# A fused attention and FFN kernel: TensorE's loop boundary moved behind a projection, two tiles of the next x treated during the value projections, the last set's blocks kept apart

## The reference

```python
q = xn @ Wq;  gate = softmax(xn @ Wg)                       # Wq 512 x 128, three heads
for i in range(3):
    k, v = xn @ Wk[i], xn @ Wv[i]
    w = sigmoid(decay_logits[i]) ** max(s - t - 1, 0) * (s > t)
    blended += gate[..., i:i+1] * (((q @ k.T) * w) @ v)
s = blended @ Wo * out_scale                                 # 128 -> 512
h = silu(xn @ W_gate.T) * (xn @ W_up.T)                      # 512 -> 1376, weights from a table of 16 values
g = silu(h @ W_down.T)                                       # 1376 -> 512
out = x + s * g
```

## Time and profile before

| what | value |
|---|---|
| median of three runs | 1935.36 us |
| profiled execution, its own time | 1939.05 us |
| its span | 1937.2 us |
| TensorE matmul busy | 1826.7 us, 94% |
| VectorE, ScalarE, GpSimd busy | 66%, 41%, 53% |
| mean granted TensorE clock | 0.987 |
| start of groups 4 and 6 (both g = 0) | 586.56 us, 811.62 us |

### The profile page before, as it was taken

How to read it: one execution, slowest core, us unless ns; L and a number is a source line. 1 busy time by engine, 2 the same in 40 slices (tenths; PEclk the granted TensorE clock), 3 DMA queues, 4 the chain that set the end, 5 groups by cost and what they waited for, 6 DMA issues and landing times. The chain is left out here.

```text
span 1937.2 us, 45221 instructions
## 1 busy us (share of the span) xinstructions
PE 1826.7 (94%) x15944; PEld 1421.2 (73%) x15944; DVE 1287.3 (66%) x2629; ACT 803.3 (41%) x1445; POOL 1025.4 (53%) x1041
## 2 busy tenths in 40 slices
PE   6899999999999999899999999999999999999997
PEld 2337878687886878688776878768786887878786
DVE  7867657475865857476674758657574866748574
ACT  3773444343443343343443434333443434444342
POOL 9204728274562827447281745628283573828353
PEclk9999999999999999999999999999999999999999
DMA  9966666758675675757666686856767676676653
GB/s 227 350 241 165 176 183 164 191 162 225 157 184 165 172 199 159 212 154 186 184 164 176 162 221 157 195 159 172 198 160 204 157 195 183 161 195 164 184 152 106
DMA packets 401850, 354.53 MB, mean 183 GB/s; under 512 B 221553, under 2 KB 277617, under 8 KB 401537
## 3 DMA queue, kind: packets, MB, share of 16 engines
q1 hardware_dynamic: 390608, 344.57, 65.7%
q0 software_dynamic: 11008, 6.89, 2.4%
HBM read 277.56 MB, written 35.52 MB: 162 GB/s over the span
## 5 line engine op out<-in xcount | busy, mean ns | idle before, releaser
L1846 PE MATMUL F<-xtc,ring 128*128 128x256 f16 (+1 forms) x4224 | 501.2, 273 | 1.5 <-DVE region L1498 1.5
L1846 PEld LDWEIGHTS F<-xtc,ring 128*128 128x128 f16 (+1 forms) x4224 | 416.5, 100 | 45.9 <-DVE region L1498 3.5
L1846 PE MATMUL F<-xt,ring 128*128 128x256 f16 (+1 forms) x3168 | 385.8, 273 | 47.6 <-DVE region L1486 47.6
L1885 PE MATMUL F<-ring,region 128*128 128x256 f16 x3360 | 392.2, 277 | 0.0
L1846 PEld LDWEIGHTS F<-xt,ring 128*128 128x128 f16 (+1 forms) x3168 | 307.2, 100 | 92.7 <-DVE region L1486 60.0
L1885 PEld LDWEIGHTS F<-ring,region 128*128 128x128 f16 x3360 | 333.4, 99 | 52.9
L823 POOL TENSOR_TENSOR region<-hs,region 128x1024 f16<-128x1024 f32 x80 | 175.4, 2193 | 63.2 <-ACT region L909 63.2
L839 POOL TENSOR_TENSOR x_sb<-x_sb,region 128x512 f32<-128x512 f32 x64 | 81.0, 1265 | 192.0 <-DVE region L1585 192.0
L1731 PE MATMUL B<-xt,a_hi 128*128 128x512 f16 x512 | 158.4, 392 | 22.2 <-issue 17.5
L785 POOL TENSOR_TENSOR rstd<-var,nhalf 128x4 f32<-128x4 f32 x15 | 15.3, 1019 | 280.2 <-DVE var L1174 280.2
L909 ACT ACTIVATE region<-region 128x256 f16<-128x256 f32 x192 | 94.4, 500 | 166.5 <-DVE region L1518 166.5
(11 more groups left out here) (272 smaller groups left out, 3466.3 us busy)
## 6 DMA issues: line engine op xcount, KB each, us to landing
ring<-blocks SPq DMA_DIRECT2D x546, 256.0 KB, 3.1
ring<-dblocks SPq DMA_DIRECT2D x224, 256.0 KB, 3.1
x_sb<-in_x SPq DMA_DIRECT2D x64, 256.0 KB, 3.3
out_y<-x_sb SPq DMA_DIRECT2D x64, 256.0 KB, 3.5
ring<-blocks SPq DMA_DIRECT2D x112, 128.0 KB, 2.5
ring<-dblocks SPq DMA_DIRECT2D x112, 128.0 KB, 2.7
blocks<-ring SPq DMA_DIRECT2D x35, 256.0 KB, 8.0
x_sb<-codes SPq DMA_DIRECT2D x10, 512.0 KB, 9.2
```

Of the source, the lines that this page charges most:

```text
L1846: ins = T_.matmul(out_, a, b, start=fresh, stop=False, skip_group_check=True)
L1885: ins = T_.matmul(bank[:, j * HV:(j + 1) * HV], a, b, start=fresh, stop=False, skip_group_check=True)
```

## The change

1. **TensorE's order.** The four q and k projections become a function `queries_keys`. Those of the first group stand ahead of the loop; in the loop body, the next iteration's stand at the end. The instructions and their order are the same; the backward branch now lies between the k projections and the v projections instead of between the down projection and the q projection.
2. **ScalarE's table.** At the head of each g = 0 group a copy of one column (`warm`) that waits for nothing.
3. **The next x.** Tiles 0 and 1 are normalised by VectorE behind the value tiles t = 1 and t = 3, copied by ScalarE at the same places, and GpSimd has `x_low(0)`, `x_low(1)`, `x_sums(0)` at the head of its group. ScalarE's `x_sums_high(0)` moves from n = 20 to n = 3, GpSimd's low sums from n = 22 to n = 5, the transposes from n = 15 and 17 to 8 and 10. The v scratch moves from `xp` to the blend buffer.
4. **Attention's places.** The first scores, masked scores, low part and retrieval come one product later; the second mixing moves from 18 to 20, its row scaling from 36 and 38 to 27.
5. **The last set.** Its u4, c12, silu2 and c22 write to blocks of their own (YB, ZB), so h2 of set 4 moves behind c22 of set 5, ScalarE's `high2(4)` behind `silu1(5)`; `h_sums_high(s)` moves from p5 of set s + 1 to p0 of set s + 2; GpSimd's `low2(5)` goes ahead of the low sums of set 4.

```diff
-        SCORES = {2: 0, 12: 1, 24: 2, 34: 3}
-        RETRIEVE = {6: 0, 17: 1, 29: 2}
-        PROBS = {3: 0, 13: 1, 25: 2}
-        LOWPR = {4: 0, 14: 1, 26: 2}
-        MIX = {11: 0, 18: 1}
+        SCORES = {3: 0, 12: 1, 24: 2, 34: 3}
+        RETRIEVE = {7: 0, 17: 1, 29: 2}
+        PROBS = {4: 0, 13: 1, 25: 2}
+        LOWPR = {5: 0, 14: 1, 26: 2}
+        MIX = {11: 0, 20: 1}
-        ROWS1 = {16: 0, 36: 1}
-        ROWS2 = {17: 0, 38: 1}
-        BLEND = {20: 0, 41: 1}
+        ROWS1 = {16: 0, 27: 1}
+        ROWS2 = {17: 0, 27: 1}
+        BLEND = {20: 0, 30: 1}
-        XHAT = {10: 0, 12: 1}
-        XLOW = {11: 0, 13: 1}
-        XPOSE = {15: 0, 17: 1}
-        XSUM = {16: 0}
-        XSUMHI = {20: 0}
-        XSUMLO = {22: 0}
+        XHAT = {1: 0, 3: 1}
+        XPOSE = {8: 0, 10: 1}
+        XSUMHI = {3: 0}
+        XSUMLO = {5: 0}
@@ GpSimd, group
+                if not last:
+                    x_low(0)
+                    x_low(1)
+                    x_sums(0)
                 for n in range(NPG):
...
+                low2(ND)
                 h_sums_low(ND - 1)
                 low1(ND)
-                low2(ND)
@@ ScalarE, group
+                if g == 0:
+                    copy(warm[:, :], dlog[:, 0:1])
...
                     copy(vb_hi[:, t], vb32[:, :]).then_inc(s_vbh, 1)
+                    if t in XHAT and not last:
+                        act.wait_ge(s_dwr[ND - 1], 16)
+                        x_high(XHAT[t], gi * GT + GT + XHAT[t] + 1)
...
                         first_copy(s)
+                        if s >= 2:
+                            h_sums_high(s - 2)
...
                     if p == 4:
                         silu1(s)
+                        if s == ND:
+                            high2(s - 1)
                     if p == 5:
                         silu2(s)
-                        if s:
+                        if s == ND:
                             h_sums_high(s - 1)
@@ VectorE, group
+                    if t in XHAT and not last:
+                        if XHAT[t] == 0:
+                            dve.wait_ge(s_tt, (gi * 2 + 2) * NTT)
+                            dve.wait_ge(s_xlo, gi * GT + GT)
+                        xhat_tile(1 - g, gi + 1, XHAT[t])
...
+                    if s == ND:
+                        dve.wait_ge(s_hl2, q - 1 + 2 * FREE)
-                    V_.tensor_tensor(ZC[0:M, 0:w], pair(2, s), YC[0:M, 0:w], ALU.add).then_inc(s_c22, 1)
+                    V_.tensor_tensor(ZB[s][0:M, 0:w], pair(2, s), YB[s][0:M, 0:w], ALU.add).then_inc(s_c22, 1)
...
                     if p == 3:
                         c22(s)
+                        if s == ND:
+                            h2(s - 1)
@@ TensorE
+            queries_keys(0, 0)
             with pe.Fori(0, NB - 1) as i:
-                for g in range(GPB):
-                    group(i, g, False)
-            for g in range(GPB):
-                group(NB - 1, g, g == GPB - 1)
+                group(i, 0)
+                queries_keys(i, 1)
+                group(i, 1)
+                queries_keys(i + 1, 0)
+            group(NB - 1, 0)
+            queries_keys(NB - 1, 1)
+            group(NB - 1, 1)
```

More of the change, by code:

```diff
@@ L251, in attention_ffn_kernel @@
         oscale = sb("oscale", [P, 1], F32)
+        warm = sb("warm", [P, 1], F32)
         fade_q = sb("fade_q", [P, NH], F32)
@@ L325, in attention_ffn_kernel @@
         C11, P5, C12, C22, C21 = cb[:, 0], cb[:, 2], cb[:, 3], cb[:, 4], cb[:, 1]
+        YB = [YC] * ND + [XC[ND % 2][:, 1:2]]
+        ZB = [ZC] * ND + [SC[ND % 2][:, 1:2]]
         attn = at["qk"].rearrange("p (t v) -> p t v", t=GT)
@@ L330, in attention_ffn_kernel @@
         pr_half = at["ph"].bitcast(F16).rearrange("p (s t) -> p s t", s=2)
-        vb32 = xp[:, 0, 0:HD]
+        vb32 = at["bl"][:, 0:HD]
         n_oh = UNR * CG * CG * BANK // 2
@@ L1045, in silu2 @@
                     act.wait_ge(s_c12, q + 1)
[L1046 removed]
+                    nc.scalar.activation(YB[s][0:M, 0:w], YB[s][0:M, 0:w], ACT.Silu,
                                          scale=f_down[0:M, LUT:LUT + 1]).then_inc(s_sg2, 1)
@@ L1080, in group @@
                         first_copy(s)
+                        if s >= 2:
+                            h_sums_high(s - 2)
                         if s:
                             high1(s - 1)
-                    if p == 1 and s:
+                    if p == 1 and 0 < s < ND:
                         high2(s - 1)
@@ L1095, in group @@
                         high_probs(PROBS[n])
-                    if n in XHAT and not last:
-                        act.wait_ge(s_dwr[ND - 1], 16)
-                        x_high(XHAT[n], gi * GT + GT + XHAT[n] + 1)
                     if n in XSUMHI and not last:
@@ L1480, in u4 @@
                     dve.wait_ge(s_u2, q + 1)
-                    if s:
+                    if s == 0:
+                        dve.wait_ge(s_yr, gi * GT + FREE)
+                    elif s < ND:
                         dve.wait_ge(s_h2, q)
-                    else:
-                        dve.wait_ge(s_yr, gi * GT + FREE)
                     dve.wait_ge(s_pp, gi * NPG + s * NP + 3)
-                    V_.tensor_tensor(YC[0:M, 0:w], pair(3, s), XC[s % 2][0:M, 0:w], ALU.add).then_inc(s_u4, 1)
+                    V_.tensor_tensor(YB[s][0:M, 0:w], pair(3, s), XC[s % 2][0:M, 0:w], ALU.add).then_inc(s_u4, 1)
                 def c22(s):
@@ L1517, in h2 @@
                     dve.wait_ge(s_sg2, q + 1)
-                    V_.scalar_tensor_tensor(out=SC[s % 2][0:M, 0:w], in0=YC[0:M, 0:w], scalar=f_hf[0:M, 0:1],
-                                            in1=ZC[0:M, 0:w], op0=ALU.mult, op1=ALU.mult).then_inc(s_h2, 1)
+                    V_.scalar_tensor_tensor(out=SC[s % 2][0:M, 0:w], in0=YB[s][0:M, 0:w], scalar=f_hf[0:M, 0:1],
+                                            in1=ZB[s][0:M, 0:w], op0=ALU.mult, op1=ALU.mult).then_inc(s_h2, 1)
                 for n in range(NPG):
@@ L1527, in group @@
                         u2(s)
-                        if s:
+                        if 0 < s < ND:
                             h2(s - 1)
@@ L1549, in group @@
                         low_probs(gi, LOWPR[n])
-                    if n in XHAT and not last:
-                        j = XHAT[n]
-                        if j == 0:
-                            dve.wait_ge(s_vbl, gi * GT + GT)
-                        xhat_tile(1 - g, gi + 1, j)
                 c21(ND)
@@ L1779, in retrieve, with queries_keys @@
                 ins.then_inc(s_pu, 1)
-            def group(i, g, last):
+            def queries_keys(i, g):
                 gi = i * GPB + g
@@ L1795, in group @@
                                       xh[:, k], xl[:, k]) for k in range(KC)], GRP).then_inc(s_pqk, 1)
+            def group(i, g):
+                gi = i * GPB + g
+                xh, xl = xt_hi[:, g], xt_lo[:, g]
                 for t in range(GT):
```

5 lines of the change are left out of this document (1 added, 4 removed).

## The result

Four runs of the changed kernel took 1968.21 to 1975.31 us, median 1971.34; four of the kernel before, beside them, 1935.11 to 1942.34, median 1937.10. The ratio is 1.0174, 95% interval 1.0143 to 1.0204: slower by 34 us. The profiled execution took 1968.21 us, 29.2 more than the one of before, and its span is 1966.3 us, 29.1 more.

A forecast was written before the change was run, and what follows sets the result against it. TensorE, its matmuls busy 94% of the span, was taken as the bound. Terms of +51.1, +10.5, -16.3 and -26.3 us gave +19 us on a 1935.4 us median, so 1954 us, range 1908 to 1980.

The forecast's parts named there:

- x tiles in the value projections: Value projections to set 1: normalising x there makes silu1(0) late and delays p0 of set 1; +49 us.
- boundary: Backward branch between groups: the stall only moves ahead of v, set 0 starting within 0.3 us of before; +2 us.
- new low clock: p0 of set 1: the new idle time is followed by the low clock in seven of 15 groups; +10.5 us.
- u4 and c12 in sets 3 and 4: Sets 3 and 4: TensorE's waits for u4 and c12 all go; -16.3 us.
- set 5: p5 and down projection: the 2.09 us wait for u4 goes, a shorter wait for low2(5) comes; -26.3 us.
- tiles hidden: p0 of set 1: x_sums_high(0) comes early enough that silu1(0) isn't late; 1906 us, chance 0.2.
- Nothing is removed from TensorE ... then the branch and its low clock ahead of v: Loop boundary: same matmuls and branch, so stall and low clock only move ahead of v; set 0 within 0.3 us.
- branch hidden behind the projection: Loop boundary: instructions fetched during the third projection's wait remove stall and low clock six times; -26 us, 1928 us, chance 0.06.
- What is late next is GpSimd: Down projection's first chunk piece: it waits 1.4 us for GpSimd's low2(5), limiting each group's gain to 1.05 us plus low clock.

The follow-up runs named there:

- Experiment 3: The changed kernel with ScalarE's x_sums_high(0) at n = 5 instead of 3 and GpSimd's low sums at n = 8 instead of 5: 1932.90 us.
- experiment 1: The kernel before with only the loop part added, the next group's q and k projections ahead of the branch: 1920.24 us, ratio 0.9897.
- experiment 5: The kernel before with the loop part, early table load and last set's part, x tiles and attention's places as before: 1912.46 us, ratio 0.9883.
- experiment 8: experiment 5 with TensorE's branch behind the value projections instead of the k projections: 1910.17 us, ratio 0.9869.
- experiment 4: The changed kernel with GpSimd's low sums of set 4 behind low1(5) and the last masked scores' low part: 1966.44 us, ratio 1.0125.
- Experiment 2: The kernel before with only the last set's own blocks, later h2(4) and high2(4), and low2(5) ahead of set 4's low sums: 1930.93 us, ratio 0.9969.
- experiment 10: experiment 8 with GpSimd's low sums of set 4 behind the last low part and SyncE's blend transposes ahead of the next x's: 1891.37 us, ratio 0.9802.
- experiment 7: The changed kernel with tiles 0 and 1 of x, their sums and transposes back in their old places: 1944.78 us, ratio 1.0059.
- experiment 9: The changed kernel with ScalarE's h_sums_high back at p5 of the next set for every set: 1957.46 us, ratio 1.0127.
- experiment 11: experiment 10 with the second mixing at n = 20 instead of 18 and the first x sums' split at 22 and 24: 1884.55 us, ratio 0.9765.
- experiment 6: experiment 5 with ScalarE's high part of the last masked scores ahead of its high part of set 4's sums: 1927.39 us, ratio 0.9966.

## Why the prediction was right in its total and wrong in two steps

The kernel became slower, as forecast, and the time lies in the stated range: 1954 us forecast, 1971 measured. That the total came so near is luck: two steps failed, one by some 20 to 29 us and the other by 19 the opposite way, and they offset each other. By the prediction's own terms, in TensorE's waits and stays at the low clock (12 before, 10 after, 1.7 us each):

| term | forecast | measured in the profiled executions |
|---|---|---|
| x tiles in the value projections | +49 | silu1 28.3, `first_copy` 12.3, u4 0.6, v_lo 13.8 - 0.7: +54 |
| boundary | +2 | issue 1.1 - 17.5, q 2.2 - 4.7, five stays at 1.7: -27 |
| new low clock | +10.5 | ten stays: +17 |
| u4 and c12 in sets 3 and 4 | -16.3 | -16.3 |
| set 5 | -26.3 | u4 -32.8, seven stays -11.9, `low2(4)` and `low2(5)` 15.4 - 1.5, low part +16.4, transposes 7.2 - 0.3: -7.5 |
| sum | +19 | +20 |

The span grew by 29.1 us. The 9 us that the table lacks lie in no row of the view of waits: from 140 us on, TensorE's idle time grew by 25.7 us, where the rows sum to 23.4, and its busy time by 3.4 us in spite of two fewer stays. They are the stops themselves. Behind 140 us the view counts 111 stops instead of 78, and the timeline has 19 more of under 0.15 us, which the view leaves out, with 1.9 us of idle time. Each of these 52 further stops costs the tail told above: 52 x 0.164 = 8.5 us, an estimate from the rows, and with the 1.9 us some 10 us, for the 9 missing. So a change that spreads the same wait over more stops costs more than its rows say.

**The x tiles: right.** Counted from the start of set 0, the second xhat was forecast to end at 6.0 us (496.8 - 490.83) and ended at 5.8; silu1(0) at 13.9 and ended at 13.7; p0 of set 1 at 13.9 and started at 13.8. VectorE's turn on ScalarE, the four sums in 4.0 us, and `x_sums_high` directly ahead of silu's table are in the timeline as described. A group with g = 1 pays 4.0 us from start to start, 4.1 forecast. Experiment 3 shows the chain to be the cause, and that two products' delay is enough. In g = 0 part of the v_lo waits isn't the tiles': experiments 1 and 5 have 4.4 and 9.9 us without them. These belong to the boundary, so the tiles cost some 44 to 50 us by the rows. The rival "tiles hidden" fell.

**The boundary: wrong.** The failed step is "Nothing is removed from TensorE ... then the branch and its low clock ahead of v". I read the constant 2.6 to 3.0 us as proof that the stall can't be covered. All six had the same 256-column pieces ahead, so the rows could not tell a stall that nothing covers from one that the same queue covers in part each time. The rival "branch hidden behind the projection", to which I gave 0.06, is what happened; experiment 1 shows it alone, 17 us by its medians and 20 by its ratio, and experiment 8 has the stall between the two sizes when matmuls of a size between are queued. ScalarE's branch, taken at 2.8 us, cost nothing that a row shows; VectorE's, which I had left out, delays q's split by 1.8 us in group 4, and TensorE waits 1.14 us for it. As that rival's price I gave 26 us; with the 4.4 to 9.9 us for v_lo counted here, the boundary gave 17 to 23, which is what experiment 1 has.

**New low clock: the mechanism too strong at one place, missed at others.** Seven stays of 1.5 us were forecast behind silu1's stall; there were two, of 1.7 us, and eleven in experiment 4 with the same stalls, so no run supports one number. Six lie behind the v_lo stalls of g = 0 (393, 850, 1079 and 1307 us, two of them twice as long), two behind the 1.02 us for the low part.

**Sets 3 and 4: right**, to the last row.

**Set 5: wrong in size.** The waits at p5 and the low clock behind them went as forecast, and TensorE waits for `low2(5)` 0.70 us at the first chunk piece, where I had 1.4, and for `low2(4)`, which I had not, 0.28 ahead of it. The failed step is the sentence "What is late next is GpSimd": I followed `low2(5)` alone and not what else the swap on GpSimd moves. The 2.12 us instruction that had run from 555.63, before the last masked scores, now starts with them, and they take 2.79 us. That is 16.4 us, and the transposes behind it 6.9. By the table the last set's part gave 7.5 us instead of 26.3. Experiment 2 has both waits without the rest of the change; experiment 4 removes one and grows the other; experiment 10 removes both.

**The 17 us between 1954 and 1971.** From the profiled execution's forecast of 1958 the miss is 10 us. Boundary and set 5 miss by -29 and +19, tiles and clock by +5 and +6.5, and 9 us are the larger number of stops. The other 7 us are where the profiled executions lie: 3.7 us above the median before, 3.1 below it after.

Experiments 5, 7 and 9 split the whole differently: by the medians the loop and the last set's blocks give 21 us; the later `h_sums_high` and the attention's places take 32 back (9 to 11 of them shown for `h_sums_high` on the full change; the places alone were not tried); the tiles with their sums at n = 3 take 27, most of it by the low clock. Together that is 38 us where the full change measured 34; the sets of runs differ by that much.

## What to carry to other kernels

Try the backward branch behind the longest instructions that can be queued ahead of it (17 to 20 us here), and then look for the engine whose branch is late next: experiment 8, with shorter ones, came out the same in total. When an instruction is moved on GpSimd, ask which VectorE instruction it will now lie beside, since a long one draws out a short one whose wait is on the path. A step that stands ahead of a table load and of the activation that frees a bank can be dear: here two places later in the hand-written order were worth 38 us. When waits are added up, count the stops too.

## What the runs showed of the hardware

- At the backward branch of this loop TensorE idled 2.6 to 3.0 us in the kernel before. In the kernel after VectorE idled 2.8 to 4.0 us there and began q's split 0.6 to 1.8 us after its input was there; in experiment 11 it idled up to 5.8 us. Between SyncE's last store and its next load lay 3.2 to 3.7 us in the two kernels. ScalarE had 0.02 us between its last silu and the table load in the kernel after.
- TensorE's stall at its branch was smaller behind wider queued matmuls: 2.6 to 3.0, 1.3 to 1.6 and 0 to 0.9 us at 256, 387 and 512 columns.
- A VectorE instruction of 128x384 (float32 in, float16 out) takes 0.55 us alone (experiment 6) and 2.8 us when a GpSimd instruction of 128x1024 starts 0.26 us behind it (the kernel after); one of 128x128 takes 0.29 us and, in experiment 4, 1.75 us. The first ended 0.4 us behind the GpSimd instruction, the second 0.1 us.
- In the kernel after, 2.3 us without matmuls were followed by the 1.2 GHz level in two of eleven cases, 1.02 us in two of sixteen, 2.24 to 2.96 us of v_lo in four of four; in experiment 4 the 2.3 us were in eleven of fifteen.
- A matmul of 256 columns is listed with 0.27 us and followed by the next after 0.11 us; the difference is added to the cost of every stop and is in no row of idle time.
